# The first product of y in each half, state times C: from VectorE to a scaled copy on ScalarE

## The reference

```python
def step(h, inp):
    d_l, B_l, C_l, x_l = inp
    A_bar = jnp.exp(d_l[:, :, None] * A)
    h = h * A_bar + (d_l * x_l)[:, :, None] * B_l[:, None, :]
    y_l = jnp.einsum('ben,bn->be', h, C_l)
    return (h, y_l)
_, ys = jax.lax.scan(step, h0, xs)
y_apply_D = y + x * W_D
y_skip = y_apply_D * _silu(skip)
```

## Time and profile before

| | us |
|---|---|
| median of 3 runs (2826.59 to 2828.7) | 2828.54 |
| the profiled execution | 2828.89 |
| its span | 2827.1 |
| PE busy | 2625.4 (93%) |
| DVE busy | 2464.6 (87%) |
| POOL busy | 2391.6 (85%) |
| ACT busy | 1878.3 (66%) |

### The profile page before, as it was taken

How to read it: one execution, slowest core, us unless ns; L and a number is a source line. 1 busy time by engine, 2 the same in 40 slices (tenths; PEclk the granted TensorE clock), 3 DMA queues, 4 the chain that set the end, 5 groups by cost and what they waited for, 6 DMA issues and landing times.

```text
span 2827.1 us, 51682 instructions
## 1 busy us (share of the span) xinstructions
PE 2625.4 (93%) x17415; PEld 2029.6 (72%) x17415; DVE 2464.6 (87%) x3218; ACT 1878.3 (66%) x4340; POOL 2391.6 (85%) x2029
## 2 busy tenths in 40 slices
PE   5777899999999999999999999999999999998868
PEld 4565677777878777786777778687777778776635
DVE  6478899999999999999999989998999999898872
ACT  6374767676676767667676776667676766767541
POOL 1158899999898999999898999989999899999781
PEclk9888899999999999999999999999999999999889
DMA  7012223223222322222222222322222222222220
GB/s 271 30 55 64 59 65 76 54 61 79 62 72 60 80 50 70 70 62 72 64 74 61 75 62 58 77 60 71 59 78 58 61 74 66 72 59 76 48 69 16
DMA packets 95311, 194.41 MB, mean 69 GB/s; under 512 B 12685, under 2 KB 32713, under 8 KB 94537
## 3 DMA queue, kind: packets, MB, share of 16 engines
q0 software_dynamic: 20736, 75.51, 13.8%
q1 hardware_dynamic: 74312, 115.60, 13.0%
HBM read 106.66 MB, written 8.91 MB: 41 GB/s over the span
## 4 chain that ended last, share of the span: by engine, by line
POOL 44%; PE 28%; issue 12%; DVE 7%; ACT 2%; DMA 1%; POOLq 1%; DVEq 0%; ACTq 0%
POOL h L778 25%; PE ps L1597 9%; POOL h L795 7%; PE ps L1608 5%; POOL hl L884 5%; PE ps L1620 5%; PE ps L1554 3%; DVE h L1343 3%; PE ps L1669 3%; POOL delta L849 2%; POOL u L892 2%; DVE xc L1401 1%; PE ps L1630 1%; POOL h L784 1%; DMA xw<-h 1%
## 5 line engine op out<-in xcount | busy, mean ns | idle before, releaser
L778 POOL TENSOR_TENSOR h<-u,bb 128x1024 f32<-128x1024 f32 x512 | 1258.4, 2468 | 33.2 <-DVE u L1418 15.4
L1343 DVE TENSOR_TENSOR_SCAN h<-ps,h 128x512 f32<-128x512 f32 x1024 | 1191.2, 1206 | 51.1 <-POOL h L784 28.3
L1037 ACT ACTIVATE ps<-delta,a_neg 128x255 f32<-128x255 f32 x2048 | 873.0, 468 | 388.3 <-DVE h L1343 386.2
L1597 PE MATMUL ps<-xh,q_up 128*128 128x256 f16 x2048 | 467.3, 275 | 31.9 <-DVE xl L1280 19.0
L1597 PE MATMUL ps<-xh,q_gate 128*128 128x256 f16 x2048 | 465.5, 274 | 13.7 <-DVE xw L1434 13.3
L1365 DVE SCALAR_TENSOR_TENSOR y<-ps,ccur,y 128x512 f32<-128x512 f32 x672 | 466.8, 736 | 7.2 <-PE ps L1554 6.4
L1597 PE MATMUL ps<-xl,q_up 128*128 128x256 f16 x2048 | 467.1, 275 | 0.0
L1597 PE MATMUL ps<-xl,q_gate 128*128 128x256 f16 x2048 | 465.5, 274 | 0.0
L1554 PE MATMUL ps<-ident,h 128*128 128x128 f32 x2944 | 397.3, 278 | 63.5 <-DVE y L1365 59.4
L1554 PEld LDWEIGHTS ps<-ident,h 128*128 128x128 f32 x2944 | 344.2, 143 | 126.2 <-DVE h L1343 59.1
L884 POOL TENSOR_TENSOR hl<-act,hh 128x512 f16<-128x512 f32 x256 | 314.9, 1230 | 102.2 <-ACT hh L1064 99.6
(11 more groups left out here) (127 smaller groups left out, 3677.2 us busy)
## 6 DMA issues: line engine op xcount, KB each, us to landing
xw<-h POOLq DMA_DIRECT2D x144, 512.0 KB, 4.5
bb<-b_scratch SPq DMA_DIRECT2D x224, 256.0 KB, 3.1
cplane<-c_scratch SPq DMA_DIRECT2D x144, 128.0 KB, 3.1
xs<-in_L_attn_resid_dram SPq DMA_DIRECT2D x17, 512.0 KB, 3.6
out_dram<-xs SPq DMA_DIRECT2D x15, 512.0 KB, 4.3
wraw<-in_L_ffn_W_up_dram SPq DMA_DIRECT2D x4, 1024.0 KB, 9.6
wraw<-in_L_ffn_W_gate_dram SPq DMA_DIRECT2D x4, 1024.0 KB, 12.3
wraw<-in_L_ffn_W_down_dram SPq DMA_DIRECT2D x4, 1024.0 KB, 14.1
```

What stands on the lines that cost most here:

```text
L778: ins = pl.tensor_tensor(hs, u[:, :, :], bb[:, q % 2, s % PLANES:s % PLANES + 1, :].broadcast_to([P, HE, CH]), ALU.mult)
L1037: ins = ac.activation(abar[r][:, e, 1:], delta[:, k, 1:], ACT.Exp, scale=a_neg[:, k, n:n + 1])
L1343: v.tensor_tensor_scan(hr, abar[r].rearrange("p e t -> p (e t)"), hr, 0.0, ALU.mult, ALU.add).then_inc(scanned, 1)
L1597: ins = te.matmul(pp[:, f * CH:(f + 1) * CH], w[:, d, col:col + P], part[:, d, :], start=(d == 0 and part is xh), stop=(d == DB - 1 and pa ...
```

## The change

The two L1362 instructions of a half leave DVE. ACT does the same product as a copy with a per-partition scale. It stands in slots 5 and 21 behind the carry of the step scanned last and ahead of hh and of all that the slot has besides; FIRST_LATE is empty, so the other place in the slot is never used. The waits that y_add had for C and for the YT jobs move with it. The other y products stay on DVE, and wait for y_added as before.

```diff
+FIRST_LATE = []
@@ ACT
+            def y_first(ph, i, s):
+                half, n, rows = s // N, state_of(s), rows_before(i, s)
+                need(sc, c_copied, i + 1)
+                if half == 1 or ph in ("loop", "last"):
+                    for q in (2 * (1 - half), 2 * (1 - half) + 1):
+                        bk, before = job_no(ph, i, f"YT_{q}")
+                        need(sc, bank_ready[bk], before + 1)
+                for t in range(TB):
+                    need(sc, hT_ready, 2 * rows + t + 1)
+                    ac.activation(y[:, t, :], hT[:, t, :], ACT.Copy, scale=ccur[:, t, n:n + 1]).then_inc(y_added[t], 1)
...
                     if step:
                         save_carry(*step)
+                    done = step_of(ph, i, s - 1)
+                    if done and done[1] % N == 0 and s not in FIRST_LATE:
+                        y_first(ph, *done)
                     if scan and s == DELAY:
                         copy_c(i)
                     for kind, p in hidden_units(ph, s):
                         hidden_high(ph, i, kind, p)
...
                     if after(ph, "D2_3", 2, s):
                         first_decay(i, 1)
+                    if done and done[1] % N == 0 and s in FIRST_LATE:
+                        y_first(ph, *done)
@@ DVE
-                if s == 0:
-                    need(ve, c_copied, i + 1)
-                if s % N == 0 and (half == 1 or ph == "loop" or ph == "last"):
-                    for q in (2 * (1 - half), 2 * (1 - half) + 1):
-                        bk, before = job_no(ph, i, f"YT_{q}")
-                        need(ve, bank_ready[bk], before + 1)
-                if is_elem(i, s):
+                if is_elem(i, s) or s % N == 0:
                     return
...
-                    if s % N == 0:
-                        ins = v.tensor_scalar(yy, hT[:, t, :], cc, None, ALU.mult)
```

More of the change, by code:

```diff
@@ L1345, in y_add @@
             def y_add(ph, i, s):
-                S, half, n = STEPS * i + s, s // N, state_of(s)
-                if s == 0:
-                    need(ve, c_copied, i + 1)
-                if s % N == 0 and (half == 1 or ph == "loop" or ph == "last"):
-                    for q in (2 * (1 - half), 2 * (1 - half) + 1):
-                        bk, before = job_no(ph, i, f"YT_{q}")
-                        need(ve, bank_ready[bk], before + 1)
-                if is_elem(i, s):
+                n = state_of(s)
+                if is_elem(i, s) or s % N == 0:
                     return
@@ L1360, in y_add @@
                     cc = ccur[:, t, n:n + 1]
-                    if s % N == 0:
-                        ins = v.tensor_scalar(yy, hT[:, t, :], cc, None, ALU.mult)
[L1363 to L1366, removed]
+                    need(ve, y_added[t], rows)
+                    v.scalar_tensor_tensor(out=yy, in0=hT[:, t, :], scalar=cc, in1=yy, op0=ALU.mult,
+                                           op1=ALU.add).then_inc(y_added[t], 1)
             def hidden_up(ph, i, kind, p):
```

## The result

| | before | after |
|---|---|---|
| median of 4 runs | 2827.57 | 2845.04 |
| lowest to highest | 2825.68 to 2828.70 | 2843.45 to 2846.32 |
| span of the profiled execution | 2827.1 | 2844.5 |

The change makes the kernel slower by 0.6%: the ratio is 1.006, with a 95% interval of 1.0048 to 1.0073. The median is 3.0 us above the 2842.0 that was predicted, and inside the range.

The account below looks back on a forecast made before the run. PE, DVE and POOL were near full, with the chain on POOL or PE at slot 5 and DVE or POOL at slot 21. Terms 8.2 + 2.2 + 0.7 + 3.9 - 1.3 = 13.7 us gave 2842 us, range 2831 to 2852.

Parts of the forecast that it names:

- The pair's price: Slots 5 and 21: the two added ACT copies of a half hold ACT for about 1.17 us.
- Slot 5, DVE and POOL: DVE's wait for tanh grows from 2.38 to some 3.9 us; POOL's late hh costs seven chunks 1.17 each, 8.2 us.
- Slot 5, chunks 1, 5, 9 and 13: Chain on PE, whose transposes wait 0.56 us for ACT's y copies: 4 x 0.56 = 2.2 us.
- in the others the chain is on PE: Slot 5: outside the seven chunks with their chain on POOL, PE carries it, so POOL's 1.17 us delay was not charged.
- dearer: Rival: all 14 chunks pay 1.17 at slot 5 and 0.40 at slot 21, 22 us, 2851; chance 0.15.
- Slot 5, chunks 4, 8 and 12: The pair comes 0.3 us earlier, so PE waits 0.25 us for y: 3 x 0.25 = 0.7 us.
- Slot 21: DVE's L1410 waits for the late conv tanh: seven chunks lose 0.15 us, seven 0.40, 3.9 us in sum.
- the cover: Slot 21: time from the conv tanh's end until DVE needs it, 1.05 us in one kind of chunk, 0.81 in the other.
- Chunk 0, half 1: L1362 is on the chain with no conv tanh behind it, so moving it gains 1.3 us.
- taking DVE's own row as the path: Chunk 0, half 1: L1362 stands on the chain on DVE, so its removal was booked as -1.3 us.
- Chunk 15 and the drain: Chunk 15 has neither hidden products nor conv beside half 0, so 0 us was booked.
- its two end figures of 10 and 24 us: Whole-kernel loss if the pair holds ACT for 0.98 us (about 10) or 1.6 us (about 24).

Follow-up runs that it names:

- the padding: Kernel before, DVE's products kept, plus four small dependent ACTIVATEs on ACT where the pair stood: 2849.39 us in slot 5, 2838.42 us in slot 21.
- the tanh's experiment: Kernel before with only half 1's first product on ACT, behind hh and the conv tanh of slot 21: 2823.06 us.
- the swap: Kernel before with one edit: in slot 21 DVE adds YT_1 ahead of the convolution's product: 2828.16 us.
- the two halves alone: Kernel before with one half's first product on ACT, placed as in the change: half 0 2842.19 us, half 1 2831.63 us.
- half 0 alone: Kernel before with only half 0's first product (slot 5) on ACT, placed as in the change: 2842.19 us.
- swap and both: Kernel before with YT_1's add ahead of the convolution's product, half 0's pair at slot 5's head, half 1's behind the conv tanh: 2819.25 us.

## Why the prediction was nearly right

- **The pair's price.** 1.17 us predicted, 1.13 and 1.14 measured, 679 ns each where the tanh had 682. Right.
- **Slot 5, DVE and POOL.** 3.9 us predicted for DVE's wait, 3.84 measured; "over 1 us" for hl, 1.32 measured. The seven chunks with their chain on POOL paid 1.15 each, and the period from chunk 1 to chunk 14 grew from 162.8 to 163.9 us. Right.
- **Slot 5, chunks 1, 5, 9 and 13.** Predicted 0.56 each; they paid 1.15, some 2.4 us more in all. The step that failed is "in the others the chain is on PE": true of the trace before, but POOL had almost no room behind PE there. Of the pair's delay of 1.16 us these chunks paid 1.15, and still 1.1 thirteen steps on, and of the padding's 1.61 they paid 1.5 to 1.6, so the room was some 0.1 us. PE's wait for y, which was there (0.28 us idle and transposes of 1.15 us), was covered by that. The padding shows it without a y. The rival "dearer" had this half of its mechanism right. The prediction did not ask how far behind the second engine is.
- **Slot 5, chunks 4, 8 and 12.** 0.25 predicted, 0.36 measured, but not for the reason given. PE's transposes L1563 wait for ACT's y in slot 5 of the eleven other loop chunks (0.25 to 0.28 us each) and in none of these three. The padding's delay less a cover of 0.8 us gives about the same price without a y. So this term came out near its size by luck.
- **Slot 21.** 0.15 and 0.40 us predicted by kind of chunk, and so measured; L1419 waits 1.36 us in chunk 10. Right, and the padding and the tanh's experiment confirm that the cover is what counts.
- **Chunk 0, half 1.** Predicted -1.3, measured 0. The step that failed is taking DVE's own row as the path: its next product was already held by POOL, 2.62 us in place of 1.21 in the trace before.
- **Chunk 15 and the drain.** Booked at 0, measured 2.7, as far as that is the change's own (see the last section). From the last pair of scans to the end of the span it is 2827.1 - 2749.53 before and 2844.5 - 2764.23 after, 77.6 and 80.3 us. The last scans of before and of after, from DVE's timelines:

```profile
2749.53 2.33 DVE L1343 TENSOR_TENSOR_SCAN h<-ps,h 128x512 f32<-128x512 f32 x2
```

```profile
2764.23 2.33 DVE L1361 TENSOR_TENSOR_SCAN h<-ps,h 128x512 f32<-128x512 f32 x2
```

Together, by the steps measured: 11 x 1.15 + 3 x 0.36 + 3.7 + 0 + 2.7 = 20.1 us. The two traces differ by 17.4, 2.7 us less. Two stretches account for that to within 0.2 us: 1.8 are there before the first y product (the scans of chunk 0 begin at 160.77 before and at 158.92 after), and 1.1 come in chunk 10, in a stretch that the trace of before has longer, as it does against the traces of the padding and of the swap. So the forecast of 13.7 missed three terms, 6.4 us (2.4 in chunks 1, 5, 9 and 13, 1.3 in chunk 0, 2.7 at the end), and differences between the two executions that the change isn't known to cause gave 2.9 of it back: part of the nearness of 2842 to 2845 is luck. Redone by the prediction's own rules, its two end figures of 10 and 24 us come to about 9 and 26; nothing hangs on them. The medians differ by 17.5, the two halves alone add up to 18.4.

## What to carry to other kernels

An operation moved to an engine with low busy share is paid for at its place in that engine's queue: read there how long each thing behind it can be late, and put it behind the last one that is waited for, or into idle time ahead. When a delay hits two engines that share the lead, the one that is second in the trace can be the one that charges for it. Before booking time that an engine gets free, look whether its next instruction is already longer than elsewhere: 1.21, 1.34 and 2.62 us for one shape meant that another engine held it.

## What was not expected of the hardware

- The exclusion of DVE's and POOL's products of SBUF operands shows in no wait of the profile: it lengthens the instruction that is held (1.21 to 4.19 us on DVE, 1.25 to 1.84 on POOL), and the view of the waits stays silent.
- In the drain PE's clock fell in other places. The output product's stretch, windows of the kernel before and of the kernel after:

```profile
2762.00:2770.00 8.00, 7.90 (x18) 3.41 (x19) 1.39 (x2) 0.00 (x0) 1.15 (x1) 1.00 0.00 0
```

```profile
2777.10:2785.10 8.00, 7.90 (x15) 3.17 (x14) 1.39 (x2) 0.00 (x0) 0.74 (x1) 0.79 0.00 0
```

  The number behind POOL's busy time is the granted clock: 1.00, 2.4 GHz throughout, before, and 0.79, part of the time at 1.2 GHz, after; 15 matmuls stand there for 18 in the same 8 us. All three kernels that delay slot 5 (the change, half 0 alone, the padding in slot 5) have 80.3 us behind the last scan, against 77.6 before. But swap and both, which delays nothing in slot 5, has 79.6 too. From 8 to 16 us behind its last scan it shows:

```profile
2746.71:2754.71 8.00, 5.96 (x9) 2.08 (x9) 1.29 (x2) 0.00 (x0) 2.48 (x2) 0.71 0.21 41
```

  In that stretch the same four traces have a granted clock of 0.71 and 9 matmuls, and the eight others, with 77.4 to 78.2 us behind the last scan, 0.81 to 0.89 and 12. So the loss goes with PE's clock in the drain and not with the delay in slot 5 alone. There is one trace of each kernel, and no run isolated why the clock was late, so that stays open, and with it whether the change is to be charged for the 2.7 us.
